# The last two query tiles of an attention kernel: three pairs of PSUM banks for their transposes, and their products and projection in places of their own ahead of tiles 12 and 13

## What is computed

```python
qkv = jnp.einsum('bsd,ed->bse', x, Wqkv)
logits = jnp.einsum('bqhd,bkhd->bhqk', q, k) * D ** (-0.5)
w = jax.nn.softmax(logits.astype(jnp.float32), axis=-1).astype(logits.dtype)
out = jnp.einsum('bhqk,bkhd->bqhd', w, v).reshape(B, S, H * D)
return jnp.einsum('bse,de->bsd', out, Wout)
```

## Time and profile before

| | us |
|---|---|
| median of 3 runs | 1910.93 |
| lowest, highest | 1906.85, 1912.75 |
| the profiled execution, its own time | 1910.57 |
| its span, first to last instruction | 1908.7 |
| around the span | 1.87 |

### The profile page before, as it was taken

One profiled execution on the slowest core, in us unless ns is written; L12 is line 12 of the kernel. 1 busy time (PEld: TensorE's weight loads), 2 busy tenths in 40 slices (PEclk: granted clock), 3 DMA queues, 4 the chain that ended last, 5 costly groups with the idle time before them and its releaser, 6 DMA issues.

```text
span 1908.7 us, 33423 instructions
## 1 busy us (share of the span) xinstructions
PE 1862.1 (98%) x11588; PEld 1665.3 (87%) x11588; DVE 1594.4 (84%) x2088; ACT 1252.2 (66%) x1700; POOL 1347.9 (71%) x514
## 2 busy tenths in 40 slices
PE   5989999999999999999999999999999999999998
PEld 4868888898888989888888988888898988889887
DVE  6368888888888889888888988888898888888885
ACT  4337676666767666666767667676766667676665
POOL 2418687776868777686877768687776868776685
PEclk9999999999999999999999999999999999999999
DMA  3037677676767767676776767677676767767664
GB/s 106 0 74 177 160 168 170 153 175 156 175 159 170 172 153 172 160 173 156 175 171 154 171 160 172 158 175 171 154 171 160 169 161 171 175 147 171 156 159 128
DMA packets 195830, 298.65 MB, mean 156 GB/s; under 512 B 37888, under 2 KB 57024, under 8 KB 195776
## 3 DMA queue, kind: packets, MB, share of 16 engines
q1 hardware_dynamic: 195776, 298.01, 66.7%
HBM read 12.65 MB, written 2.10 MB: 8 GB/s over the span
## 4 chain that ended last, share of the span: by engine, by line
PE 79%; POOL 6%; SPq 5%; issue 4%; DVE 3%; ACT 1%; DMA 1%; POOLq 0%; DVEq 0%; ACTq 0%
PE ps_o L371 30%; PE ps_s L362 10%; PE ps_s L363 10%; PE ps_s L364 10%; SPq L279 5%; POOL parts L1035 4%; PE ps_t L352 4%; PE ps_s L333 4%; PE ps_t L342 4%; PE ps_s L405 2%; PE ps_o L380 1%; PE ps_o L382 1%; PE ps_o L381 1%; DVE prob L891 1%; DMA raw<-prob 1%
## 5 line engine op out<-in xcount | busy, mean ns | idle before, releaser
L1035 POOL TENSOR_TENSOR parts<-raw,parts 128x2048 fp32r<-128x2048 f32 x254 | 1175.7, 4629 | 443.6 <-ACT parts L669 443.5
L681 ACT ACTIVATE prob<-ps_s,neg_max 128x1024 f32<-128x1024 f32 x512 | 567.0, 1114 | 449.0 <-DVE neg_max L885 448.8
L881 DVE TENSOR_REDUCE row_max<-ps_s 128x1 f32<-128x1024 f32 x512 | 613.0, 1213 | 114.1 <-PE ps_s L364 95.7
L891 DVE STREAM_TRANSPOSE prob<-prob 128x1024 f32<-128x1024 f32 x508 | 599.5, 1218 | 60.7 <-ACT prob L681 60.3
L669 ACT CAST parts<-raw 128x2048 fp32r<-128x2048 f32 x254 | 486.3, 1915 | 105.8 <-DMA raw<-prob 104.3
L371 PE MATMUL ps_o<-parts,v_hi 128*128 128x256 f32 x4064 | 515.8, 280 | 4.8 <-POOL v_lo L1028 4.8
L371 PEld LDWEIGHTS ps_o<-parts,v_hi 128*128 128x128 f32 x4064 | 497.9, 189 | 20.5 <-POOL v_lo L1028 6.1
L362 PE MATMUL ps_s<-k_hi,q_hi 128*128 128x512 f32 x1024 | 402.6, 393 | 12.5 <-ACT prob L681 11.5
L363 PE MATMUL ps_s<-k_lo,q_hi 128*128 128x512 f32 x1024 | 400.3, 391 | 0.0
L364 PE MATMUL ps_s<-k_hi,q_lo 128*128 128x512 f32 x1024 | 400.1, 391 | 0.0
L371 PE MATMUL ps_o<-parts,v_lo 128*128 128x256 f32 x2032 | 275.6, 278 | 0.0
(11 more groups left out here) (111 smaller groups left out, 1571.6 us busy)
## 6 DMA issues: line engine op xcount, KB each, us to landing
raw<-prob SPq DMA_DIRECT2D x2032, 128.0 KB, 2.4
v_raw<-v_turned SPq DMA_DIRECT2D x244, 64.0 KB, 2.0
w_raw<-wqkv_dram SPq DMA_DIRECT2D x32, 128.0 KB, 2.5
y<-x_dram SPq DMA_DIRECT2D x4, 512.0 KB, 6.1
wo_raw<-wqkv_dram SPq DMA_DIRECT2D x16, 128.0 KB, 2.5
wo_raw<-wo_dram SPq DMA_DIRECT2D x16, 128.0 KB, 2.3
out_dram<-y SPq DMA_DIRECT2D x8, 256.0 KB, 2.7
w_raw<-w_dram SPq DMA_DIRECT2D x2, 704.0 KB, 10.6
```

What stands on the lines that cost most here:

```text
L681: nc.scalar.activation(tile, logit, ACT.Exp, bias=neg_max[:, t:t + 1], scale=SCALE, accum_out=row_sum[:, t, half:half + 1]).then_inc(s_exp, 1)
L881: nc.vector.reduce_max(row_max[:, t, half:half + 1], ps_s[:, 2 * half:2 * half + 2, :].rearrange("p b n -> p (b n)"), AX_X).then_inc(s_mx, 1)
L891: nc.vector.transpose(tile, tile).then_inc(s_xp, 1)
L1035: nc.gpsimd.tensor_tensor(half_of(0, half), moved(p, half), half_of(1, half), ALU.subtract).then_inc(s_pl, 1)
```

## The change

It touches only what comes after the last logits of the last head.

- `last_turned(n)` gives group 0 banks 0 and 1 of `ps_s`, group 1 banks 2 and 3, group 2 the two banks of `ps_t`, and group 3 banks 0 and 1 of `ps_s` again. Group 2 waits for nobody; group 3 waits for the subtraction of group 0.
- `ps_last` is now in bank 2 of `ps_s`, so `products_last(0)` waits for the subtraction of group 1.
- Pair 7 gets its own `last_o_hi` and `last_o_lo` (room of the query weights in `w_sp`), its own bank for the projection (`ps_y_last`, bank 3 of `ps_s`), and semaphores.
- On PE, `products_last(0)` goes ahead of the projection of pair 5, `products_last(1)` ahead of the second half of pair 6, and the projection of pair 7 ahead of that of pair 6.
- On ACT, `last_high(0)` goes ahead of the cast of pair 6's first half and `last_high(1)` behind it; the cast of pair 7's output goes ahead of that of pair 6. On DVE, the subtraction and the result of pair 7 go ahead of those of pair 6.
- SP stores pair 7 ahead of pair 6, and pair 6 as two DMAs of one tile each, one behind each addition.

```diff
-        ps_last = ps_t[:, 0, 0:2 * P]
+        ps_last = ps_s[:, 2, 0:2 * P]
+        ps_y_last = ps_s[:, 3, :]
+        last_o_hi, last_o_lo = [w_sp[:, 0, c].rearrange("p w d -> p (w d)") for c in range(C)]
...
         def last_turned(n):
-            return ps_s[:, n % 2 * 2:n % 2 * 2 + 2, :].rearrange("p b (k q) -> p (b k) q", q=2 * P)
+            banks = (ps_s[:, 0:2, :], ps_s[:, 2:4, :], ps_t[:, :, :], ps_s[:, 0:2, :])[n]
+            return banks.rearrange("p b (k q) -> p (b k) q", q=2 * P)
...
-            for p in range(PAIRS):
+            for p in range(PAIRS - 2):
                 sp.wait_ge(s_yacc, T * H + 2 * p + 2)
                 sp.dma_start(out_v[:, 2 * p:2 * p + 2, :], y[:, 2 * p:2 * p + 2, :]).then_inc(s_out, 16)
-            sp.wait_ge(s_out, 16 * PAIRS)
+            sp.wait_ge(s_yacc_last, 2)
+            sp.dma_start(out_v[:, T - 2:T, :], y[:, T - 2:T, :]).then_inc(s_out, 16)
+            for t in (T - 4, T - 3):
+                sp.wait_ge(s_yacc, T * H + t + 1)
+                sp.dma_start(out_v[:, t, :], y[:, t, :]).then_inc(s_out, 16)
+            sp.wait_ge(s_out, 16 * (PAIRS + 1))
...
-            for n in (2, 3):
-                pe.wait_ge(s_llo, n - 1)
-                turn_last(n)
+            turn_last(2)
+            pe.wait_ge(s_llo, 1)
+            turn_last(3)
+            pe.wait_ge(s_llo, 2)
+            products_last(0)
             output_step(end, 5)
             product_step(end, 6, 0)
-            products_last(0)
-            product_step(end, 6, 1)
             pe.wait_ge(s_llo, 4)
             products_last(1)
+            product_step(end, 6, 1)
+            pe.wait_ge(s_olo_last, 1)
+            out_projection(ps_y_last, last_o_hi, last_o_lo, s_y_last)
             output_step(end, 6)
-            output_step(end, 7)
...
-                    if t % 2:
+                    if final and t == T - 1:
+                        last_high(0)
+                        high(h, 6, 0, True)
+                        last_high(1)
+                    elif t % 2:
...
-            last_high(0)
-            last_high(1)
             output_high(end, 5)
             high(end, 6, 1, True)
             last_high(2)
             last_high(3)
+            act.wait_ge(s_lpv, 2)
+            nc.scalar.copy(last_o_hi, ps_last).then_inc(s_ohi_last, 1)
             output_high(end, 6)
-            act.wait_ge(s_lpv, 2)
-            act.wait_ge(s_y, count(8, end, 7))
-            nc.scalar.copy(o_hi[:], ps_last).then_inc(s_ohi, 1)
...
             result(end, 5)
+            dve.wait_ge(s_ohi_last, 1)
+            nc.vector.tensor_tensor(last_o_lo, ps_last, last_o_hi, ALU.subtract).then_inc(s_olo_last, 1)
             output_low(end, 6)
+            dve.wait_ge(s_inv, count(8, end, 8))
+            dve.wait_ge(s_y_last, 1)
+            add_result(7, ps_y_last, s_yacc_last)
             result(end, 6)
-            dve.wait_ge(s_ohi, count(8, end, 8))
-            nc.vector.tensor_tensor(o_lo[:], ps_last, o_hi[:], ALU.subtract).then_inc(s_olo, 1)
-            result(end, 7)
```

More of the change, by code:

```diff
@@ L233, in build @@
         s_lpv = sem("last_products_done")
+        s_ohi_last = sem("last_output_high_ready")
+        s_olo_last = sem("last_output_low_ready")
+        s_y_last = sem("last_projection_done")
+        s_yacc_last = sem("last_result_added")
         s_y = sem("projection_done")
@@ L374, in products, with out_projection @@
                 last.then_inc(s_pv, 1)
-            def out_projection(p):
+            def out_projection(to, o_hi, o_lo, done):
                 for j in range(2):
                     tile = slice(j * P, (j + 1) * P)
-                    dst = ps_y[:, j * DIM:(j + 1) * DIM]
+                    dst = to[:, j * DIM:(j + 1) * DIM]
                     nc.tensor.matmul(dst, o_hi[:, tile], wo_hi[:], start=True, stop=False)
@@ L382, in out_projection @@
                     last = nc.tensor.matmul(dst, o_lo[:, tile], wo_hi[:], start=False, stop=True)
-                last.then_inc(s_y, 1)
+                last.then_inc(done, 1)
             def transpose_x(g):
@@ L470, in output_step @@
                 pe.wait_ge(s_yacc, count(16, h, 16 + 2 * p))
-                out_projection(p)
+                out_projection(ps_y, o_hi, o_lo, s_y)
             def head(h, first, final):
@@ L904, in inverse, with add_result @@
                 nc.vector.reciprocal(inv_denom[:, 2 * p:2 * p + 2], denom[:, 2 * p:2 * p + 2]).then_inc(s_inv, 1)
+            def add_result(p, src, added):
+                for j in range(2):
+                    t = 2 * p + j
+                    nc.vector.scalar_tensor_tensor(out=y[:, t, :], in0=src[:, j * DIM:(j + 1) * DIM],
+                                                   scalar=inv_denom[:, t:t + 1], in1=y[:, t, :],
+                                                   op0=ALU.mult, op1=ALU.add).then_inc(added, 1)
             def result(h, p):
@@ L908, in result @@
                 dve.wait_ge(s_y, count(8, h, p + 1))
-                for j in range(2):
-                    t = 2 * p + j
-                    nc.vector.scalar_tensor_tensor(out=y[:, t, :], in0=ps_y[:, j * DIM:(j + 1) * DIM],
-                                                   scalar=inv_denom[:, t:t + 1], in1=y[:, t, :],
-                                                   op0=ALU.mult, op1=ALU.add).then_inc(s_yacc, 1)
+                add_result(p, ps_y, s_yacc)
             origin = (0, 0)
```

## The result

| | before | after |
|---|---|---|
| median of 20 runs, us | 1910.93 | 1907.42 |
| lowest, highest, us | 1906.85, 1912.75 | 1904.14, 1909.86 |
| the profiled execution, us | 1910.57 | 1905.24 |
| its span, us | 1908.7 | 1903.4 |

The change makes the kernel 3.5 us faster. The ratio of the times is 0.9982, with a 95% interval of 0.9976 to 0.9989: a gain of 2.1 to 4.6 us. It is real, and the ratio of the medians is still within the 0.3% that the prediction took for its bound.

What follows compares the result with a forecast made beforehand. PE was taken to bound the kernel, leaving only the last 27 us at stake. Gains of 3.07 us to DVE's end and 0.25 from the store make 3.3, so 1910.57 - 3.3 = 1907.3 us, range 1904.5 to 1911.0.

Steps and rivals of the forecast that it cites:

- Group 2: Last transposes on PE: writing to `ps_t` without a wait, it starts at 1886.34 and not 1887.99, 1.65 us earlier.
- The loss of 0.1 us in front of `products_last(0)`: PE waits for `last_low(1)`, ending at 1887.98, so the group effectively starts at 1888.14 rather than 1888.03.
- ACT's order: ACT casts `last_high(0)` at 1883.0 to 1884.0, in the time in which it waited for the DMA.
- The cover of pair 7's output: Pair 7's `o_hi` and `o_lo` run under the second half of pair 6, with 1.7 us to spare.
- The 0.3 us of idle ahead of the last projection: PE idles some 0.3 us until pair 6's `o_lo` ends at 1901.08; the last projection starts at 1901.14.
- The gain up to DVE's end: The last additions on DVE end at 1903.10 where they ended at 1906.17, a gain of 3.07 us.
- The store: Last store of 128 KB lands 1.9 us behind DVE's end instead of 2.13: gain 0.25 us, bounds none to 0.45.
- Rival (a): Three stores close together at the end land late, gain falls to 1.8 us: 1908.8 to 1909.3 us; chance 0.08.
- Rival (b): ACT's new order holds pair 6's cast and POOL; a cast 1.5 us late gives 1908.8 us; chance 0.06.
- Rival (c): Added instructions lengthen the 16 heads: 0.21 us each eats the 3.3 us, 0.5 each gives 1915.3 us; chance 0.08.
- Rival (d): Run scatter moves a median by 2 us either way; 0.16 for passing the lower end, out of the forecast's 0.78.
- the sum: Whole tail: 3.07 us to DVE's end plus 0.25 from the store, 3.3 us in all, bounds 2.0 to 3.5.

Runs made afterwards that it cites:

- the second comparison: The unchanged kernel with the change, run again beside the kernel before on one chip: 1906.39 us against 1910.52, ratio 0.9980 (0.9970 to 0.9990).
- The second trace: Trace of the same kernel with the change, run again unedited: first transposes at 1883.78 us, tail 23.5 us, median 1906.39 us.
- The store kernel: The change with tiles 12 and 13 of pair 6 in one 256 KB store behind both additions: tail 23.9 us against 23.6.

## Why the prediction was right

Forecast 1907.3 us, measured 1907.42. That the two agree to 0.1 us is luck: the interval of the gain is 2.1 to 4.6 us, and the second comparison gave 4.1. What the traces bear out is the way there, 3.2 us of tail for a forecast of 3.3. Each time below is counted from the first transposes.

| step | predicted | in after |
|---|---|---|
| group 2 starts | 4.43 | 4.60 |
| group 3 | 5.28 | 5.47 |
| `products_last(0)` | 6.23 | 6.26 |
| projection of pair 5 | 9.09 | 9.21 |
| `products_last(1)` | 12.55 | 12.67 |
| second half of pair 6 | 15.41 | 15.53 |
| projection of pair 7 | 18.15 | 18.27 |
| last projection | 19.23 | 19.35 |
| end of the last addition | 21.19 | 21.32 |
| end of the span | 23.5 | 23.6 |

- **Group 2** was 0.17 us late, since the 24 products of pair 5 took 2.91 us and not the 2.74 of the earlier trace rows. The second trace has 4.53, so part of it varies. The 2.74 us are those of pair 6, and the trace of before had the difference: for pair 5, behind transposes, the first 16 products take 2.13 us, and for pair 6, in the timeline of 1880.5 to 1912 us:

```profile
1890.77 1.99 PE L371 MATMUL ps_o<-parts,v_hi 128*128 128x256 f32 x16
```

- **The loss of 0.1 us in front of `products_last(0)`** did not come as a wait: PE's row there has no bracket. With group 2 late, the subtraction, which ended 6.08 us behind the first transposes, was in time. But this group took 2.95 us (1886.10 to 1889.05) and not 2.86; it follows transposes too, and its first 16 products took 2.15 us, the later ones of pair 7 2.06. Why products behind transposes are slower is not shown. These terms together leave the 0.1 us by which every later step is late.
- **ACT's order** as what hides this seam was right as a mechanism. The prediction gave it no size; by the kernel that undid it it is 1.0 to 1.3 us.
- **The cover of pair 7's output** held: `o_lo` ready 1.7 us before PE came, as predicted. The 0.3 us of idle ahead of the last projection was 0.2 to 0.4. The gain up to DVE's end was 24.26 - 21.32 = 2.94 us for 3.07.
- **The store**: 2.24 us from DVE's end to the end of the span, for 2.53 before, a gain of 0.29 us where I took 0.25. The store kernel shows that the size is what did it. The prediction called the 2.1 us of before lower than the fixed part of the Trainium skill's fit; they are 0.1 us above its 2.0, and 0.5 us below the 2.6 that is the estimate by the fit for 256 KB.
- **Rival (a), the store turns worse**: it did not. Landings were 1.8 us for the tiles and 2.2 for pair 7. The argument against it, that each of the three finds the DMA engines idle, was wrong and went against the prediction's own walk: the data of tile 12 follow those of pair 7 in one piece. It cost nothing in after, and when the stores moved closer a tile took 2.1 us.
- **Rival (b), pair 6's parts late**: PE had no wait for POOL in front of either half of pair 6.
- **Rival (c), longer heads**: the starts of the change, 1879.84 and 1883.78, lie on both sides of those of before, 1880.78 and 1881.91. By the row maxima, heads 2 to 13 take 1330.8 and 1331.0 us in the two traces of before and 1330.8 and 1330.6 in those of the change. Nothing is added per head, and the 5.9 us between the runs, which the prediction spread over the heads as 0.37 us each, are not in these twelve: they vary by 1.0 us together.
- **Rival (d), scatter**: it moved the median by 0.2 us against the sum's 3.3 us. In the profiled pair, though, it was 2.07 of 5.3 us. Whoever had compared the two spans alone would have found 60% more gain than there is.

What the prediction didn't say is how little most parts are worth one by one: nothing for the banks, 1.0 us with the first products and ACT's order, 0.3 less than that with the second products as well, 1.0 for own places, and 3.2 to 3.4 together.

## What to carry to other kernels

In the tail of a program, take PE's list as a chain of producers and consumers and move the consumer, its producers' order on ACT and its buffers in one step; here the buffers of the transposes alone only moved PE to the next waits. Compare tails from a common event and not by the ends of two profiled spans, since the part before it can scatter by as much as the gain. Within the tail, look too whether a DMA landed later before giving a few tenths to an edit. Where a pipeline fills and TensorE waits in short gaps, look at the granted clock there: idle slots can take matmuls that nobody reads.

## What the runs showed of the hardware

- At the start of head 0 the granted clock fell to 0.50 (1.2 GHz) for about 7 us in all in 13 of 13 traces, though the longest wait of PE there was 3.0 us. Filling PE's waits removed it: 1.00 in the trace, and a mean clock of 0.999 in 8 of 8 executions.
- At the end of the program with idles of 0.9 and 1.4 us, six matmuls apart, the clock fell to 0.50 in one execution, 0.75 us into the second idle, and stayed at 1.00 in the next of the same kernel. A projection of six matmuls took 1.65 us by the lower clock and 0.98 by the higher.
- Stores from SBUF issued by SP landed in 2.1 to 2.2 us for 256 KB at the end of the program. Two of 128 KB, issued 0.8 and 1.2 us behind one of 256 KB, landed in 1.7 to 1.8 us, and in 2.0 to 2.1 us when issued 0.4 and 0.9 us behind it.
- The first 16 products of a group of pair 5 or 6 took 2.08 to 2.13 us behind transposes and 1.99 to 2.00 behind other matmuls with no wait between, those of pair 7 2.15 to 2.18 and 2.06 to 2.07.
